# Expert stage of a decoder layer: the sum of row names moves from VectorE to GpSimd, and scatters lose one of their waits

## The chip, the core and the metric

The kernel runs on one core of a Trainium2 chip. Its engines are TensorE (PE), VectorE (DVE), ScalarE (ACT), GpSimd (POOL) and SyncE (SP, which only issues DMAs here). Each runs its own instructions in order, and they wait for each other through semaphores. The metric is the time of one execution on the device in microseconds (us). Before the change it is 1711.96 us, the median of three runs (1709.74 to 1717.92).

## The reference

One decoder layer on 4096 tokens (64 sequences of 64) of 256 numbers, in float32: self-attention, cross-attention with 16 heads over a context, and a mixture of experts. The change touches the last one alone:

```python
logits = x @ gate_w.T                          # 64 experts
topv, topi = jax.lax.top_k(logits, 8)
rw = softmax(topv)
gu = jnp.einsum('nh,eih->nei', x, gu_w)        # gate and up, 64 wide each
inter = silu(gate) * up * W[:, :, None]
out = jnp.einsum('nei,ehi->nh', inter, dp_w)
out = out + sigmoid(x @ sh_gate1_w.T) * shared_expert(x)
x = layernorm(x + out)
```

Only eight of 64 experts count for a token, so the kernel computes those alone.

## The kernel before

There are three stages. The attention stage goes over 32 tiles of 128 tokens. It ends each tile by routing: every token's row (its 256 numbers, its eight slot numbers, its token number times eight, its shared gate) is scattered by POOL into `slot_scratch` in DRAM, where the rows of one expert lie together. The expert stage then works through 176 steps. Of these 160 are sparse, of two tiles of 128 rows, each tile with one expert; 16 are shared, where the tokens pass the shared expert. The last stage loads, for each token, its eight results from `expert_out_scratch`, weighs and sums them and normalises. Those loads wait for all scatters.

In the expert stage each engine has its own order, written out by hand. PE in round s turns the x rows of step s (`turn_x`, L1664), multiplies by gate and up for step s-1 (`gate_and_up`, L1682), turns the gated product of s-2 (`turn_inner`, L1690) and makes the down products of s-3 (`project`, L1701 and L1703, which signal `y_ready`). ACT copies x out of PSUM (L1741), takes silu (L1748) and copies the turned product (L1756). SP loads the rows of a step eight steps ahead (L1548) and waits in `free_rows` (L1520) until the buffer is free: it wants x turned, y ready and the name taken of eight steps before.

A result row goes to the place token times eight plus the column in which the token holds this slot. DVE works that out in three parts:

- `match_row` (L1806): compares the eight slot numbers of each row with the slot that the row lies in, times the column; two instructions give `matched`.
- `name_row` (L1819): adds the token number to it, `named`, as integers.
- `bound_row` (L1825): keeps 16 bits and adds a large number for rows that the step doesn't own, so that the scatter leaves them out; this is `target`, a ring of eight.

DVE's round s is: match of s, the product of silu and up of s-1 (`gate_inner`, L1840), name of s, copy of y of s-3 out of PSUM (`copy_y`, L1849), bound of s, and in 96 of the rounds a piece of the router's weights (`find_weights`, L1859). The down products of step s wait for the copy of y of step s-1, since they write the same bank.

POOL has nothing in this stage but the scatters (`scatter`, L1617). For each sparse step it issues two indirect DMAs of 128 rows (L1623), after three waits:

```python
pool.wait_ge(sig["y_copied"], s + 1)
pool.wait_ge(sig["row_bounded"], n + 1)
pool.wait_ge(sig["y_ready"], min(s + 2, STEPS))
```

The third is the down products of step s+1. The y buffers are a ring of eight (`HELD`).

Of the kernel before, what the change touches and what calls it, by code (L numbers as in the profile page):

```python
# [11 lines left out]
ALU = mybir.AluOpType  # L12
# [3 lines left out]
P = 128  # L16
# [12 lines left out]
SLOT8, TOK, GATE = D, D + TOP_K, D + TOP_K + 1  # L29
# [11 lines left out]
SPARSE_STEPS = (N * TOP_K // P + EXPERTS) // 2  # L41
STEPS = SHARED_STEPS + SPARSE_STEPS
# [1367 lines left out]
slots_numbered slots_open  # L1410
x_in0 x_in1 x_in2 x_in3 x_in4 x_in5 x_in6 x_in7
x_turned x_copied gate_up_done silu_done gated inner_turned inner_copied y_ready y_copied
row_matched row_named row_bounded
y_stored0 y_stored1 y_stored2 y_stored3 y_stored4 y_stored5 y_stored6 y_stored7
y_scattered0 y_scattered1 y_scattered2 y_scattered3 y_scattered4 y_scattered5 y_scattered6 y_scattered7
slots_as_float w_matched w_kept w_summed
# [3 lines left out]
def expert_phase(nc, sig, end, out, slot_d, row_d, meta_d, y_d, shared_d, place_d, first_d, bound_d, count, jump, w8, gu, dp,  # L1420
                 places, rows, slot_of, weights, scattered, down):

    with ExitStack() as stack:
        def sb(name, shape, dt=F32):
            return stack.enter_context(nc.sbuf_tensor(name, shape, dt))
# [18 lines left out]
        x_in = [sb(f"x_rows{n}", [P, 2, XW]) for n in range(8)]  # L1444
# [8 lines left out]
        part = sb("part", [P, 1])  # L1453
        column = sb("column", [P, TOP_K])
        match = [sb(f"match{n}", [P, 2, TOP_K]) for n in range(2)]
        matched = [sb(f"matched{n}", [P, 2]) for n in range(2)]
        named = [sb(f"named{n}", [P, 2], U32) for n in range(2)]
        targets = sb("targets", [P, 8, 2], U32)
        target = [targets[:, n, :] for n in range(8)]
# [20 lines left out]
        steps_of = {step: s for s, step in enumerate(order)}  # L1480

        def sparse(s):
            return order[s][0] == "sparse"

        def number(s):
            return order[s][1]
# [26 lines left out]
        def _(sp):  # L1513
# [6 lines left out]
            def free_rows(s):  # L1520

                if s >= 8:
                    sp.wait_ge(sig["x_turned"], s - 7)
                    if sparse(s):
                        sp.wait_ge(sig["y_ready"], s - 7)
                    if sparse(s - 8):
                        sp.wait_ge(sig["row_named"], number(s - 8) + 1)
                    else:
                        sp.wait_ge(sig["y_copied"], s - 7)

# [71 lines left out]
        @block.gpsimd  # L1602
        def _(pool):
            nc.gpsimd.memset(identity[:, :], 0.0).then_inc(sig["identity_zeroed3"], 1)
            pool.wait_ge(sig["identity_zeroed3"], 1)
            nc.gpsimd.affine_select(out=identity[:, :], in_=identity[:, :], compare_op=ALU.not_equal, fill=1.0,
                                    base=0, pattern=[[-1, P]], channel_multiplier=1).then_inc(sig["identity_made3"], 1)
            nc.gpsimd.memset(minus_half[:, :], -0.5).then_inc(end["constants4"], 1)

            def fill(out, pattern, base, step):  # L1610
                nc.gpsimd.iota(out, pattern, base=base, channel_multiplier=step,
                               allow_small_or_imprecise_dtypes=True).then_inc(sig["numbered"], 1)

            fill(part[:, :], [[0, 1]], 0, 1)
            fill(column[:, :], [[1, TOP_K]], 0, 0)

            def scatter(s):  # L1617
                n = number(s)
                pool.wait_ge(sig["y_copied"], s + 1)
                pool.wait_ge(sig["row_bounded"], n + 1)  # L1620
                pool.wait_ge(sig["y_ready"], min(s + 2, STEPS))
                for j in range(2):
                    nc.gpsimd.indirect_dma_start(  # L1623
                        out=y_d[:, :],
                        out_offset=bass.IndirectOffsetOnAxis(ap=target[n % 8][:, j:j + 1], axis=0),
                        in_=y[s % HELD][:, j, :], in_offset=None, bounds_check=N * COLS - 1, oob_is_err=False)\
                        .then_inc(sig[f"y_scattered{s % HELD}"], 16)

            for s in range(STEPS):
                if sparse(s):  # L1630
                    scatter(s)
            for n in range(HELD):
                pool.wait_ge(sig[f"y_scattered{n}"], 32 * sum(sparse(s) for s in range(n, STEPS, HELD)))

            def root(t):
                pool.wait_ge(end["var"], t + 1)
                nc.gpsimd.tensor_tensor(rs[:, t % 4:t % 4 + 1], ve[:, t % 4:t % 4 + 1], minus_half[:, :], ALU.pow)\
                    .then_inc(end["rstd"], 1)

            pool.wait_ge(end["constants4"], 1)  # L1640
            for t in range(TILES):
                root(t)
# [146 lines left out]
        def _(dve):  # L1789
# [16 lines left out]
            def match_row(s):  # L1806
                n = number(s)
                dve.wait_ge(*rows_loaded(s))
                if n == 0:
                    dve.wait_ge(sig["slots_numbered"], 1)  # L1810
                if n >= 2:
                    dve.wait_ge(sig["row_named"], n - 1)
                for j in range(2):
                    nc.vector.scalar_tensor_tensor(match[n % 2][:, j, :], x_in[s % 8][:, j, SLOT8:SLOT8 + TOP_K].bitcast(U32),  # L1814
                                                   slot_of[:, 0, 2 * n + j:2 * n + j + 1], column[:, :], ALU.is_equal,
                                                   ALU.mult, accum_out=matched[n % 2][:, j:j + 1])\
                        .then_inc(sig["row_matched"], 1)

            def name_row(s):  # L1819
                n = number(s)  # L1820
                dve.wait_ge(sig["row_matched"], 2 * n + 2)
                nc.vector.tensor_tensor(named[n % 2][:, :], matched[n % 2][:, :], x_in[s % 8][:, :, TOK], ALU.add)\
                    .then_inc(sig["row_named"], 1)

            def bound_row(s):  # L1825
                n = number(s)
                dve.wait_ge(sig["row_named"], n + 1)
                if n == 0:
                    dve.wait_ge(sig["slots_open"], 4)
                if n >= 8:  # L1830
                    dve.wait_ge(*y_free(steps_of["sparse", n - 8]))
                nc.vector.scalar_tensor_tensor(target[n % 8][:, :], named[n % 2][:, :], 0xFFFF,  # L1832
                                               beyond[:, 2 * n:2 * n + 2], ALU.bitwise_and, ALU.bitwise_or)\
                    .then_inc(sig["row_bounded"], 1)
# [24 lines left out]
            def find_weights(n):  # L1859

                t, stage = n // 3, n % 3
                if n % (3 * META_TILES) == 0:
                    part_of = n // (3 * META_TILES)
                    dve.wait_ge(sig["metas_in"], 16 * (part_of + 1))
                    dve.wait_ge(sig["slots_in"], 16 * (part_of + 1))
                    own = slice(t, t + META_TILES)
                    nc.vector.tensor_copy(slots_f[:, own, :], slots[:, own, :]).then_inc(sig["slots_as_float"], 1)
                    dve.wait_ge(sig["slots_as_float"], part_of + 1)
                wide = [P, TOP_K, EXPERTS]
                if stage == 0:  # L1870
                    nc.vector.tensor_tensor(w_match[:, :, :], metas[:, t % (2 * META_TILES), 0:EXPERTS].unsqueeze(1).to_broadcast(wide),
                                            slots_f[:, t, :].unsqueeze(2).to_broadcast(wide), ALU.is_equal)\
                        .then_inc(sig["w_matched"], 1)
                elif stage == 1:
                    dve.wait_ge(sig["w_matched"], t + 1)
                    nc.vector.tensor_tensor(w_match[:, :, :], w_match[:, :, :],
                                            metas[:, t % (2 * META_TILES), EXPERTS:].unsqueeze(1).to_broadcast(wide), ALU.mult)\
                        .then_inc(sig["w_kept"], 1)
                else:
                    dve.wait_ge(sig["w_kept"], t + 1)  # L1880
                    nc.vector.tensor_reduce(w8[:, t, :], w_match[:, :, :], AX.X, ALU.add).then_inc(sig["w_summed"], 1)

            for s in range(STEPS + 3):
                now = s < STEPS and sparse(s)
                if now and number(s) == 0:
                    table_slots()
                if now:
                    match_row(s)
                if 0 <= s - 1 < STEPS:
                    gate_inner(s - 1)  # L1890
                if now:
                    name_row(s)
                if 0 <= s - 3 < STEPS:
                    copy_y(s - 3)
                if now:
                    bound_row(s)
                n = number(s) - 24 if now else None
                if now and 0 <= n < 3 * TILES:
                    find_weights(n)
# [88 lines left out]
```

## Time and profile before

| | |
|---|---|
| median of three runs | 1711.96 us |
| profiled execution | 1717.95 us |
| its span, first to last instruction | 1716.2 us |
| mean granted TensorE clock | 0.939 of 2.4 GHz |
| PE, DVE, ACT, POOL busy | 1461.1, 1134.9, 770.8, 1000.0 us |
| DMA | 247.99 MB, mean 144 GB/s |

The profile's page comes from one execution. An engine's busy time counts its compute instructions, and for POOL its indirect DMAs while they are issued. The attention stage takes about the first 1000 us, the expert stage runs to about 1613, the last stage to the end. "Released by" in a row is worked out from the semaphores; "remote" means that the profile doesn't name the releaser. Ends of matmuls are modelled.

### The profile page before, as it was taken

Reading aid. Unit: us, or ns where it says so; the run is one execution under the profiler, and the core shown is the slowest. Engines: PE = TensorE matmul, PEld = TensorE weight load, DVE = VectorE, ACT = ScalarE, POOL = GpSimd, SP = SyncE. Lnnn points to the kernel's source line nnn. Section 1 sums busy time; section 2 is a strip of 40 time slices with the busy share of each in tenths; the row PEclk is TensorE's granted clock in tenths of the full one; section 3 lists DMA queues with packets and bytes.
Section 4 is the critical chain, followed back from the end, with each engine's and each line's share of the span. In section 5 each row is a group of like instructions: output and inputs, shape, how many; then the busy total and the mean of one; then the engine's idle time right before and its main releaser. Section 6 shows DMA issues by size and latency. Waiting matters only on the chain. (4 is left out here: it accounts for less than half of the span.)

```text
span 1716.2 us, 35026 instructions
## 1 busy us (share of the span) xinstructions
PE 1461.1 (85%) x9324; PEld 1183.5 (69%) x9324; DVE 1134.9 (66%) x3731; ACT 770.8 (45%) x2649; POOL 1000.0 (58%) x991
## 2 busy tenths in 40 slices
PE   3799999999999999999998727877877787887587
PEld 2688888888888888888887625655655555665464
DVE  2568787878778888888887444455555555344398
ACT  2465656565565565555655112322322232232254
POOL 3446777776766776777766424455555555555322
PEclk8799999999999999999999759899899999889799
DMA  7333232323232212122212946656656556554697
GB/s 259 101 119 104 98 117 83 125 78 119 86 111 75 83 58 80 64 74 66 72 64 83 291 150 186 185 173 174 188 168 186 171 170 177 173 172 134 228 417 318
DMA packets 184341, 247.99 MB, mean 144 GB/s; under 512 B 30796, under 2 KB 160921, under 8 KB 179748
## 3 DMA queue, kind: packets, MB, share of 16 engines
q1 hardware_dynamic: 150820, 171.55, 32.7%
q0 software_dynamic: 27648, 69.28, 11.0%
q10 hardware_dynamic: 5760, 5.87, 1.0%
q8 instruction: 45, 0.74, 0.2%
q14 instruction: 68, 0.56, 0.1%
HBM read 136.98 MB, written 117.98 MB: 149 GB/s over the span
## 5 line engine op out<-in xcount | busy, mean ns | idle before, releaser
L1623 POOL DMA_INDIRECT expert_out_scratch<-y,targets x320 | 318.9, 997 | 277.2 <-DVE targets L1832 104.8
L573 POOL DMA_INDIRECT slot_scratch<-xrow x256 | 273.6, 1069 | 194.4 <-issue 90.4
L1682 PE MATMUL bank_g<-gu,x_turned 128*128 (+1 forms) x1408 | 213.6, 299 | 29.8 <-issue 18.8
L1682 PEld LDWEIGHTS bank_g<-gu,x_turned 128*128 128x128 f32 x1408 | 189.2, 209 | 48.7 <-issue 47.8
L1840 DVE TENSOR_TENSOR inter<-silu,bank_g 128x128 f32<-128x128 f32 x176 | 50.3, 286 | 256.9 <-ACT silu L1748 213.4
L1741 ACT ACTIVATE x_turned<-bank_x 128x512 f32<-128x512 f32 x176 | 105.4, 599 | 231.2 <-PE bank_x L1664 144.7
L860 ACT ACTIVATE q_work<-q_work 128x128 f32<-128x128 f32 x512 | 151.1, 298 | 128.9 <-DVE q_work L1058 110.3
L764 PE MATMUL bank_d<-wo_w,o2t 128*128 128x256 f32 x1536 | 194.5, 287 | 3.0 <-DVE o2t L977 3.0
L764 PEld LDWEIGHTS bank_d<-wo_w,o2t 128*128 128x128 f32 x1536 | 188.7, 194 | 3.1 <-DVE o2t L977 3.1
L1701 PE MATMUL bank_y<-dp,inter_t 64*128 (+1 forms) x352 | 132.8, 460 | 49.7 <-DVE y L1849 23.1
L522 POOL TENSOR_TENSOR q_rs<-q_ve,minus_half 128x8 f32<-128x8 f32 x64 | 105.5, 1648 | 89.4 <-DVE q_ve L1048 88.8
L628 PE MATMUL bank_c<-wq_w,x1t 128*128 128x512 f32 x576 | 144.3, 395 | 3.6 <-DVE x1t L977 2.8
L1664 PE MATMUL bank_x<-identity,x_rows 128*128 128x128 f32 x704 | 123.4, 301 | 25.5 <-DMA x_rows<-token_row_scratch 25.5
L1664 PEld LDWEIGHTS bank_x<-identity,x_rows 128*128 128x128 f32 x704 | 79.8, 149 | 88.8 <-issue 88.5
L1849 DVE COPY y<-bank_y 128x512 f32<-128x512 f32 x160 | 110.1, 688 | 46.2 <-PE bank_y L1703 25.8
L1748 ACT ACTIVATE silu<-bank_g 128x128 f32<-128x128 f32 x176 | 49.6, 282 | 191.5 <-PE bank_g L1682 112.9
L1703 PE MATMUL bank_y<-dp,inter_t 64*128 64x256 f32 x352 | 133.3, 461 | 0.0
L729 PE MATMUL bank_c<-k2t,stage_b 128*128 128x64 f32 x1024 | 127.1, 285 | 0.0
L628 PEld LDWEIGHTS bank_c<-wq_w,x1t 128*128 128x128 f32 x576 | 107.7, 191 | 25.5 <-DVE x1t L977 3.2
L729 PEld LDWEIGHTS bank_c<-k2t,stage_b 128*128 128x128 f32 x1024 | 123.4, 201 | 0.6 <-issue 0.3
L1701 PEld LDWEIGHTS bank_y<-dp,inter_t 64*128 64x128 f32 x352 | 56.2, 199 | 84.6 <-issue 82.2
L860 ACT ACTIVATION_READ_ACCUMULATOR q_work<-q_work 128x1 f32 x512 | 96.9, 189 | 0.0
(253 smaller groups left out, 3225.9 us busy)
## 6 DMA issues: line engine op xcount, KB each, us to landing
x_rows<-slot_scratch SPq DMA_DIRECT2D x320, 136.0 KB
results<-expert_out_scratch SPq DMA_DIRECT2D x32, 1024.0 KB, 8.8
slot_scratch<-zeros SPq DMA_DIRECT2D x16, 816.0 KB, 4.5
dp<-in_down SPq DMA_DIRECT2D x161, 64.0 KB
slot_scratch<-zeros SPq DMA_DIRECT2D x8, 1088.0 KB, 8.4
gu<-in_gate_up SPq DMA_DIRECT2D x11, 768.0 KB
expert_out_scratch<-y,targets POOLq DMA_INDIRECT x320
token_row_scratch<-xrow SPq DMA_DIRECT2D x32, 136.0 KB
```

Of the source, the lines that this page charges most:

```text
L522: nc.gpsimd.tensor_tensor(out_, base, minus_half[:, 0:width], ALU.pow).then_inc(sig[done], 1)
L573: nc.gpsimd.indirect_dma_start(out=slot_d[:, :], out_offset=bass.IndirectOffsetOnAxis(ap=xrow[slot][:, SLOT8 + k:SLOT8 + k + 1].bitcast(U3 ...
L628: last = nc.tensor.matmul(target, left[a][:, c, :], right(b, c), start=(n == 0 and c == 0), stop=(n == len(PASSES) - 1 and c == C - 1))
L729: last = nc.tensor.matmul(bank_c[:, n, p * S:(p + 1) * S], q2t[:, n, 2 * p:2 * p + 2, :].rearrange("p h s -> p (h s)"), k2t[:, p // 2, n * ...
L764: last = nc.tensor.matmul(bank_d[:, 0, 0:D], o2t[a][:, h, :], wo_w[b][:, h, :], start=(n == 0 and h == 0), stop=(n == len(PASSES) - 1 and ...
L860: last = nc.scalar.activation(q2s[:, h, :], q2[:, h, :], ACT.Square, accum_out=q2_ss[:, h:h + 1])
L1623: nc.gpsimd.indirect_dma_start(out=y_d[:, :], out_offset=bass.IndirectOffsetOnAxis(ap=target[n % 8][:, j:j + 1], axis=0), in_=y[s % HELD][ ...
L1664: mm = nc.tensor.transpose(bank_x[:, s % 2, (2 * j + c) * P:(2 * j + c + 1) * P], x_in[s % 8][:, j, c * P:(c + 1) * P], identity[:, :])
L1682: mm = nc.tensor.matmul(bank_g[:, s % 2, j * P:(j + 1) * P], xt[s % 2][:, j, c, :], w, start=(c == 0), stop=(c == C - 1))
L1701: nc.tensor.matmul(bank_y[:, 0, 0:D], inter_t[s % 2][0:INNER, :], dp[0:INNER, bass.ds(own, D)], start=True, stop=True)
L1703: nc.tensor.matmul(bank_y[:, 1, 0:D], inter_t[s % 2][INNER:P, :], dp[INNER:P, ring * D:(ring + 1) * D], start=True, stop=True).then_inc(si ...
L1849: nc.vector.tensor_copy(y[s % HELD][:, :, :], bank_y[:, :, 0:D])\
```

## The change

POOL makes the sum of token and column (`sum_row`), two sparse steps ahead of the pair that it scatters next, and signals `row_summed`. DVE's `name_row` becomes a clamp of that sum to 0..65535, and it and `bound_row` move to two rounds later. `matched` becomes a ring of eight, and there is a new ring `summed`. The scatters no longer wait for the down products of the next step. SP's `free_rows` waits for `row_summed` in place of `row_named`.

```diff
@@ free_rows (SP)
                     if sparse(s - 8):
-                        sp.wait_ge(sig["row_named"], number(s - 8) + 1)
+                        sp.wait_ge(sig["row_summed"], number(s - 8) + 1)
@@ scatter (POOL)
                 pool.wait_ge(sig["y_copied"], s + 1)
                 pool.wait_ge(sig["row_bounded"], n + 1)
-                pool.wait_ge(sig["y_ready"], min(s + 2, STEPS))
...
-            for s in range(STEPS):
-                if sparse(s):
-                    scatter(s)
+            SUMMED_AHEAD = 2
+
+            def sum_row(n):
+                if n >= SPARSE_STEPS:
+                    return
+                pool.wait_ge(sig["row_matched"], 2 * n + 2)
+                if n >= 8:
+                    pool.wait_ge(sig["row_named"], n - 7)
+                nc.gpsimd.tensor_tensor(summed[:, n % 8, :], matched[:, n % 8, :],
+                                        x_in[steps_of["sparse", n] % 8][:, :, TOK], ALU.add)\
+                    .then_inc(sig["row_summed"], 1)
+
+            for n in range(SUMMED_AHEAD):
+                sum_row(n)
+            for n in range(SPARSE_STEPS):
+                sum_row(n + SUMMED_AHEAD)
+                scatter(steps_of["sparse", n])
@@ match_row, name_row (DVE)
                 if n >= 2:
-                    dve.wait_ge(sig["row_named"], n - 1)
+                    dve.wait_ge(sig["row_matched"], 2 * n - 2)
+                if n >= 8:
+                    dve.wait_ge(sig["row_summed"], (n - 7))
...
-                                                   ALU.mult, accum_out=matched[n % 2][:, j:j + 1])\
+                                                   ALU.mult, accum_out=matched[:, n % 8, j:j + 1])\
...
-                dve.wait_ge(sig["row_matched"], 2 * n + 2)
-                nc.vector.tensor_tensor(named[n % 2][:, :], matched[n % 2][:, :], x_in[s % 8][:, :, TOK], ALU.add)\
+                dve.wait_ge(sig["row_summed"], (n + 1))
+                nc.vector.tensor_scalar(named[n % 2][:, :], summed[:, n % 8, :], 0.0, 65535.0, ALU.max, ALU.min)\
                     .then_inc(sig["row_named"], 1)
@@ find_weights (DVE)
                 if stage == 0:
+                    dve.wait_ge(sig["w_summed"], t)
@@ DVE's rounds
-                if now:
-                    name_row(s)
+                named_now = s - 2 >= 0 and s - 2 < STEPS and sparse(s - 2)
+                if named_now:
+                    name_row(s - 2)
                 if 0 <= s - 3 < STEPS:
                     copy_y(s - 3)
-                if now:
-                    bound_row(s)
+                if named_now:
+                    bound_row(s - 2)
```

## Rows read from the trace of the kernel before

**Rows 1.** L1623, the scatters: the page's part 5, then instructions and who waited.
```profile
L1623 POOL DMA_INDIRECT expert_out_scratch<-y,targets x320 | 318.9, 997 | 277.2 <-DVE targets L1832 104.8
...
L1623 POOL DMA_INDIRECT expert_out_scratch<-y,targets x320: 971/972/1383, 1035.4 to 1611.8; - x160
...
who waited for it (us, times):
```

**Rows 2.** Busy time of each engine in a window of the expert stage.
```profile
core 0: us, PE busy (x) PEld busy (x) DVE busy (x) ACT busy (x) POOL busy (x), PEclk, DMA share, GB/s
1030.00:1606.00 576.00, 455.53 (x2925) 330.37 (x2924) 286.40 (x1404) 169.31 (x516) 313.66 (x315) 0.93 0.58 171
```

**Rows 3.** Waits from 1030 to 1606 us: total, times, longest.
```profile
POOL expert_out_scratch L1623 <- DVE targets L1832: 104.8, 43, 18.7
...
POOL expert_out_scratch L1623 <- remote: 65.3, 32, 2.3
...
ACT x_turned L1741 <- remote: 36.1, 11, 6.0
...
POOL expert_out_scratch L1623 <- PE bank_y L1703: 33.7, 21, 4.2
...
POOL expert_out_scratch L1623 <- DVE y L1849: 5.1, 7, 1.8
```

**Rows 4.** Timeline of a stall: start, us, engine, line; idle before in brackets.
```profile
1203.02 0.66 PE L1664 MATMUL bank_x<-identity,x_rows 128*128 128x128 f32 x4
...
1205.21 0.97 POOL L1623 DMA_INDIRECT expert_out_scratch<-y,targets  x1 [0.30 <-issue]
1205.24 0.66 PE L1664 MATMUL bank_x<-identity,x_rows 128*128 128x128 f32 x4
...
1206.49 0.97 POOL L1623 DMA_INDIRECT expert_out_scratch<-y,targets  x1 [0.30 <-issue]
...
1208.02 0.60 ACT L1741 ACTIVATE x_turned<-bank_x 128x512 f32<-128x512 f32 x1 [5.18 <-remote]
1208.74 2.07 PE L1682 MATMUL bank_g<-gu,x_turned 128*128 x8 [2.84 <-issue]
...
1209.79 0.97 POOL L1623 DMA_INDIRECT expert_out_scratch<-y,targets  x1 [2.32 <-remote]
```

**Rows 5.** Timeline around the first pair of scatters.
```profile
1031.67 0.69 DVE L1849 COPY y<-bank_y 128x512 f32<-128x512 f32 x1
...
1034.09 0.38 PE L1703 MATMUL bank_y<-dp,inter_t 64*128 64x256 f32 x1
...
1035.39 1.00 POOL L1623 DMA_INDIRECT expert_out_scratch<-y,targets  x1 [18.75 <-DVE targets L1832]
```

**Rows 6.** Timeline around the last pair of scatters.
```profile
1605.88 0.69 DVE L1849 COPY y<-bank_y 128x512 f32<-128x512 f32 x1 [1.50 <-PE bank_y L1703]
...
1609.24 0.97 POOL L1623 DMA_INDIRECT expert_out_scratch<-y,targets  x1 [0.30 <-issue]
1610.51 0.97 POOL L1623 DMA_INDIRECT expert_out_scratch<-y,targets  x1 [0.30 <-issue]
```

**Rows 7.** POOL's instructions by form: busy us, mean ns, idle before.
```profile
L548 POOL TENSOR_TENSOR q_work<-q_work,q_rs 128x1024 f32<-128x1024 f32 x32 | 60.7, 1897 | 2.5
...
L522 POOL TENSOR_TENSOR h_rs<-h_ve,minus_half 128x1 f32<-128x1 f32 x64 | 37.7, 589 | 16.9 <-DVE h_ve L984 16.5
...
L1611 POOL IOTA part<- 128x1 f32 x1 | 0.1, 131 | 0.0
```

**Rows 8.** Two lines of DVE: ns at the least, median, most.
```profile
L1822 DVE TENSOR_TENSOR named<-matched,x_rows x160: 148/155/230, 1025.5 to 1597.4; 128x2 uint32<-128x2 f32 x160
...
L1017 DVE TENSOR_SCALAR p1n<-p,p_rec x32: 286/457/479, 32.4 to 900.4; 128x128 f32<-128x128 f32 x32
```

**Rows 9.** Timeline of a longer scatter.
```profile
1216.77 0.69 DVE L1871 TENSOR_TENSOR w_match<-metas,slots 128x512 f32<-128x512 f32 x1
1216.92 1.38 POOL L1623 DMA_INDIRECT expert_out_scratch<-y,targets  x1 [1.62 <-DVE targets L1832]
...
1218.61 0.97 POOL L1623 DMA_INDIRECT expert_out_scratch<-y,targets  x1 [0.30 <-issue]
```

More of the change, by code:

```diff
@@ L1412 @@
 x_turned x_copied gate_up_done silu_done gated inner_turned inner_copied y_ready y_copied
-row_matched row_named row_bounded
+row_matched row_summed row_named row_bounded
 y_stored0 y_stored1 y_stored2 y_stored3 y_stored4 y_stored5 y_stored6 y_stored7
@@ L1455, in expert_phase @@
         match = [sb(f"match{n}", [P, 2, TOP_K]) for n in range(2)]
-        matched = [sb(f"matched{n}", [P, 2]) for n in range(2)]
+        matched = sb("matched", [P, 8, 2])
+        summed = sb("summed", [P, 8, 2])
         named = [sb(f"named{n}", [P, 2], U32) for n in range(2)]
```

## The prediction

> **What bounds the kernel now.** I read the page first. In its second part the expert stage stands out (from about 1000 us on): PE falls from nines to sevens and eights, and DMA doubles. The costliest group of the page belongs to this stage: POOL's 320 indirect DMAs, two for each of 160 sparse steps [rows 1]. Next the stage's window from 1030 to 1606 us: POOL is busy 313.7 of 576 us, PE 455.5, DVE 286.4, ACT 169.3, and the granted clock is 0.93 [rows 2]. With 176 steps in the stage (160 sparse, 16 shared) a step takes about 3.3 us. No engine is full: PE stands still for 120.5 us, POOL for 262.3 us.
>
> Then the waits. POOL's come before the first scatter of a pair: 104.8 + 65.3 + 33.7 + 5.1 = 208.9 us in 103 of 160 pairs; ACT stands 36.1 us on something the profile doesn't name [rows 3]. The timeline shows what a stall looks like. PE's four turns of x end at 1205.90, yet ACT, which needs them alone, starts at 1208.02, 2.1 us late, and PE's next product only at 1208.74. All that time POOL runs scatters back to back; its last ends at 1207.46, the signals come through about a microsecond later, and the next pair starts at 1209.79 [rows 4]. So the stage is bound by a loop of short dependent steps over PE, ACT and DVE whose signals arrive late while POOL and its scatters are at work. Two numbers rule it: how long POOL's work covers a step, and how late each signal is.
>
> Nothing waits for POOL: the list of who waited for the scatters is empty [rows 1]. Eight y buffers and eight targets keep it free.
>
> **The wait that goes.** A pair waits for its own y (copied by DVE) and for the down products of the next step, and those products wait for the same copy, so the second event is always the later one. First pair: y's copy runs 1031.67 + 0.69 = 1032.36, the next products end at 34.09 + 0.38 = 1034.47, and the scatter starts at 1035.39, so 0.92 us after its last condition [rows 5]. Without the wait it could start at 1032.36 + 0.92 = 1033.28, 2.1 us earlier. I did this for each pair: earliest start = the later of (own copy's end + 0.92) and (end of the pair before + 0.30, the gap inside a pair). The last pair gains nothing: the pair before ends at 1610.21 and it starts at 1610.51 [rows 6]. Over pairs 2 to 160 POOL's removable idle is 130 us, in 83 pairs more than 0.3 us.
>
> That is not yet time of the kernel, since nobody waits for POOL. An earlier pair ends earlier, and so the stretch with late signals ends earlier; but that pays only where PE stands too. I take the share of PE's idle in POOL's idle, 120.5 / 262.3 = 0.46: 130 x 0.46 = -60 us. The bounds are 0 (nobody waits for POOL) and -130. At the end of the stage the results are loaded only when the last scatter has landed, and POOL runs behind: last copy ends at 1606.57, last pair starts 3.9 us later [rows 6]. With each pair earlier I take -2 us there (0 to -3.1).
>
> **The sum that POOL takes over.** 160 adds of 128x2. No such add is in the trace: a 128x1 fill takes 0.131 us, a 128x1 power 0.589, and an add or product of 128x1024 1.897 [rows 7]. I take 0.30, between the small ones, and 0.08 for its gap, as before the large products (2.5 us for 32 [rows 7]). Where POOL stood idle anyway the add lies in the idle time; where pairs ran back to back, 76 by my count, it is paid: 76 x 0.38 = +29 us. Bounds: 76 x 0.21 = +16, 160 x 0.67 = +107.
>
> **The names on DVE.** The DVE add (0.155 us) becomes a clamp of the same size [rows 8]; 0 +/- a few us, beneath DVE's 290 us of idle [rows 2]. It moves two steps later, with the bound, but still ahead of that step's copy of y, so the scatter doesn't wait for it. The new waits on match (sum of eight steps before, match of two before) and on w_summed rest on things long done, and so does SP's wait for the sum: two steps later than the name, of eight. Nothing for these. But the clamp now waits for POOL, in front of the copy of y. POOL adds for step m+3 only after it has issued the scatters of step m, and DVE copies y of step m+2 only after the clamp of m+3. That closes a circle that was open. Uncongested it takes 0.92 (copy to scatter), 2.25 (the pair [rows 4]), 0.38 (add), about 0.2 to be seen, 0.16 (clamp) and 0.69 (copy) = 4.6 us for two steps, below the 6.6 that two steps take now. I charge 40 late clamps at 0.2 = +8 us (0 to +80, as below).
>
> **The sum.** -60 - 2 + 29 + 8 = -25 us. The profiled execution took 1717.95 us (1.75 around its span of 1716.2), near the top of the three runs (1709.74 to 1717.92); it becomes 1693. On the median of 1711.96 that is 1687 us.
>
> **A rule of the skill.** Row first: the scatter that started at 1216.92, while a DVE product of two SBUF tiles ran (1216.77 to 1217.46), took 1.38 us and the next one 0.97 [rows 9]. The Trainium skill, "SBUF — State Buffer", "Who interferes with whom", says that a VectorE instruction with two SBUF inputs keeps a GpSimd one that reads SBUF out for its whole length, and that a VectorE instruction in a 2-port mode (its list has tensor_scalar, which the clamp is) and a GpSimd one shut each other out. By the first part this trace agrees; on the clamp it speaks against the change, and becomes the third rival.
>
> **Rivals.** (1) *The new circle binds: slower.* The clamp stands behind POOL's pair, and signals are late exactly then. With one signal late by 2.1 us, as in [rows 4], in place of the 0.2, the circle takes 6.5 us, or 3.25 a step, no better than now; with y's signal late by 0.5 as well 7.0, 3.5 a step: 160 x 0.2 = +32 us, 1744 us. It decides from a total lateness of some 2 us a turn. For it: POOL would need 2.25 + 0.30 + 0.38 = 2.9 us of the 3.3 of a step, so it has little room to catch up, and PE's bursts at 2.2 us a step (turns of x at 1203.02 and 1205.24 [rows 4]) would be cut. Against: in the windows where POOL is idle signals are prompt.
>
> (2) *Nothing comes of either.* Starting earlier only moves the pairs to another phase of the step: each pair is released by the copy instead of by the next products, one step on, and the same number of late signals meets the loop. Then the adds hide in the idle and it stays at 1712, within 0.5%. For it: nobody waits for POOL [rows 1].
>
> (3) *The clamp is shut out by the scatters.* The nearest rows are DVE's products by a scalar in SBUF, 0.286 us at the least and 0.457 in the median [rows 8]: +0.17 each for 160 is +27 us; at worst a whole scatter, 0.97. Half of it lies in DVE's idle, so +13 us, 1725; shut out for a whole scatter at every third step, +50.
>
> **Chances.** Forecast 0.45, rival 1 0.30, rival 2 0.15, rival 3 0.10. The likeliest case's own range is 1665 to 1703 (the 0.46 from 0.3 to 0.65). The range goes from 1650 (the gain without the costs) to 1750 (rival 1 with a little more): a case where all 130 us are gained, or where the clamp loses a scatter each time, is left out. 0.5% (8.6 us) is about what can be told from no change here: faster 0.45, same 0.18 (rival 2 and the edges of the others), slower 0.37.
>
> **What would show it.** Right: POOL's waits before a pair fall from 209 us to under 120; the pairs' first scatter follows its own copy by about 0.9 us; the add takes about 0.3 us; PE's idle in the stage falls below 100 us; the last scatter starts within 3 us of the last copy. Rival 1: the clamp's line appears with idle before it released by POOL's add, over 60 us in all, and PE's down products wait longer on the copy of y. Rival 2: PE's idle stays near 120 us though POOL's waits shift. Rival 3: clamps of 0.3 us and more, or start late with no release. Wrong altogether: if the stage's length doesn't follow PE's idle, or if the time moves in the attention stage, whose code is the same.

## The result

The change made the kernel slower: 1743.46 us (median of 4 runs, 1739.6 to 1749.75) against 1714.94 for the kernel before (4 runs, 1709.74 to 1718.53), a ratio of 1.0155 [1.0125, 1.0185]. The forecast of 1687 had the wrong sign. The range held the time, and it is the figure of the first rival almost to the microsecond, but the cause was another one, as the experiments show. The profiled execution took 1749.75 us.

The page of the changed kernel, its first part and the lines that answer to [rows 1] and to DVE's copy of y (line, engine, operation, out<-in, count; busy us, mean ns of one; idle before it and its releasers):

```profile
PE 1485.0 (85%) x9324; PEld 1203.8 (69%) x9324; DVE 1141.7 (65%) x3731; ACT 774.6 (44%) x2649; POOL 1038.8 (59%) x1151
...
L1623 POOL DMA_INDIRECT expert_out_scratch<-y,targets x320 | 319.8, 999 | 250.7 <-DVE y L1865 126.7
```

The changed kernel, the stage from the first to the last of the 160 sparse copies of y, and a window of the attention stage (columns as in [rows 2]):

```profile
1037.90:1638.80 600.90, 467.57 (x2912) 342.06 (x2912) 291.22 (x1399) 172.10 (x513) 352.40 (x473) 0.89 0.55 164
100.00:900.00 800.00, 780.23 (x5275) 677.01 (x5274) 647.35 (x1701) 463.69 (x1740) 561.91 (x527) 0.99 0.25 84
```

The same two windows of the kernel before:

```profile
1031.70:1605.90 574.20, 453.83 (x2912) 329.17 (x2911) 285.22 (x1396) 168.27 (x513) 313.56 (x315) 0.93 0.58 171
100.00:900.00 800.00, 780.20 (x5317) 677.43 (x5314) 651.56 (x1712) 462.67 (x1742) 563.28 (x528) 1.00 0.26 85
```

The attention stage is the same (PE 780.2 us in both). The spans differ by 31.8 us: the copies run over 26.7 us more, and the first one comes 6.2 us later, which is no part of the change (over the runs below it lies between 1023 and 1042 us, whatever the kernel). Of the 26.7 us, PE's idle time takes 13.0 (120.4 to 133.3) and its busy time 13.7, with the same 2912 matmul records at a lower granted clock, 0.89 for 0.93. Most of the idle time is new at one place: before the down products PE stands 78.7 us in all, where it was 49.6; before the gate products it fell from 27.7 to 13.6.

Where PE's idle time comes from stands in the waits from 1030 to 1640 us. The changed kernel (total, times, longest):

```profile
POOL expert_out_scratch L1623 <- DVE y L1865: 126.7, 58, 3.0
...
POOL expert_out_scratch L1623 <- DVE targets L1848: 53.9, 18, 4.9
...
DVE y L1865 <- remote: 46.5, 28, 3.3
PE bank_y L1715 <- DVE y L1865: 42.1, 33, 2.6
...
ACT x_turned L1755 <- remote: 40.1, 19, 3.4
...
ACT silu L1762 <- remote: 30.3, 16, 4.1
...
DVE y L1865 <- PE bank_y L1717: 27.0, 40, 2.1
...
POOL expert_out_scratch L1623 <- DVE named L1838: 2.2, 2, 1.9
```

The kernel before, the same waits around the copy of y, and ACT's before silu:

```profile
ACT silu L1748 <- remote: 63.4, 30, 3.9
...
DVE y L1849 <- PE bank_y L1703: 25.8, 39, 1.5
...
PE bank_y L1701 <- DVE y L1849: 23.1, 23, 1.8
...
DVE y L1849 <- remote: 11.5, 13, 1.7
```

POOL waits less before a pair, 126.7 + 53.9 + 2.2 = 182.8 us where [rows 3] add up to 208.9. But DVE's copy of y waits 46.5 us on something unnamed, where it was 11.5, and PE's down products wait 42.1 us for that copy, where it was 23.1. ACT's silu went the other way, 30.3 us on something unnamed where it was 63.4. The new instructions themselves, by their lines (ns at the least, median, most):

```profile
L1637 POOL TENSOR_TENSOR summed<-matched,x_rows x160: 197/218/770, 1032.0 to 1636.0; 128x2 f32<-128x2 f32 x160
its engine sat idle before it (us, times) until:
  DVE match L1830: 10.9, 3
who waited for it (us, times):
  DVE named L1838: 1.0, 1
```

```profile
L1838 DVE TENSOR_SCALAR named<-summed x160: 154/161/420, 1035.5 to 1636.2; 128x2 uint32<-128x2 f32 x160
```

DVE's clamp waited for POOL's add once, for 1.0 us: the circle of rival 1 did not bind. How an add lies between pairs (start, us, engine, line; idle before in brackets):

```profile
1200.91 1.19 POOL L1623 DMA_INDIRECT expert_out_scratch<-y,targets  x1 [0.30 <-issue]
...
1202.10 0.22 POOL L1637 TENSOR_TENSOR summed<-matched,x_rows 128x2 f32<-128x2 f32 x1
...
1202.49 1.00 POOL L1623 DMA_INDIRECT expert_out_scratch<-y,targets  x1 [0.16 <-issue]
```

From scatter to scatter 0.39 us pass (1202.10 to 1202.49) where 0.30 do without an add; over the pairs that stand back to back the median is 0.392 with an add and 0.305 without. Most of the add fits into a gap that was there, and 0.09 us of POOL's cadence is its price.

### The profile page after: what moved, and what is told of

Its sections match the earlier page's. It is cut to its first block and busy times, and to the rows that moved or that the text cites. A ratio compares the mean times of both kernels' runs of the same rounds, so it can differ in the third digit from the quotient of the medians.

```text
span 1748.0 us, 35342 instructions
## 1 busy us (share of the span) xinstructions
PE 1485.0 (85%) x9324; PEld 1203.8 (69%) x9324; DVE 1141.7 (65%) x3731; ACT 774.6 (44%) x2649; POOL 1038.8 (59%) x1151
## 5 line engine op out<-in xcount | busy, mean ns | idle before, releaser
L1623 POOL DMA_INDIRECT expert_out_scratch<-y,targets x320 | 319.8, 999 | 250.7 <-DVE y L1865 126.7
L1696 PE MATMUL bank_g<-gu,x_turned 128*128 (+1 forms) x1408 | 220.5, 307 | 15.5 <-issue 13.3
L1696 PEld LDWEIGHTS bank_g<-gu,x_turned 128*128 128x128 f32 x1408 | 197.6, 217 | 30.9 <-issue 30.3
L1715 PE MATMUL bank_y<-dp,inter_t 64*128 (+1 forms) x352 | 139.9, 482 | 78.7 <-DVE y L1865 42.1
L1865 DVE COPY y<-bank_y 128x512 f32<-128x512 f32 x160 | 110.1, 688 | 81.1 <-remote 46.5
L1717 PE MATMUL bank_y<-dp,inter_t 64*128 64x256 f32 x352 | 140.4, 483 | 0.0
L729 PEld LDWEIGHTS bank_c<-k2t,stage_b 128*128 128x128 f32 x1024 | 126.7, 205 | 0.6 <-issue 0.3
```

What stands on the lines that cost most here:

```text
L729: last = nc.tensor.matmul(bank_c[:, n, p * S:(p + 1) * S], q2t[:, n, 2 * p:2 * p + 2, :].rearrange("p h s -> p (h s)"), k2t[:, p // 2, n * ...
L1623: nc.gpsimd.indirect_dma_start(out=y_d[:, :], out_offset=bass.IndirectOffsetOnAxis(ap=target[n % 8][:, j:j + 1], axis=0), in_=y[s % HELD][ ...
L1696: mm = nc.tensor.matmul(bank_g[:, s % 2, j * P:(j + 1) * P], xt[s % 2][:, j, c, :], w, start=(c == 0), stop=(c == C - 1))
L1715: nc.tensor.matmul(bank_y[:, 0, 0:D], inter_t[s % 2][0:INNER, :], dp[0:INNER, bass.ds(own, D)], start=True, stop=True)
L1717: nc.tensor.matmul(bank_y[:, 1, 0:D], inter_t[s % 2][INNER:P, :], dp[INNER:P, ring * D:(ring + 1) * D], start=True, stop=True).then_inc(si ...
L1865: nc.vector.tensor_copy(y[s % HELD][:, :, :], bank_y[:, :, 0:D])\
```

## Experiments

**The chips.** The runs fell on chips of two kinds. On chips 3 and 4 the kernel before took 1560.82 us (median of 12 runs) and 1561.1 (of 25), on chip 14 it took 1717.09 and 1717.84 (of 13 and 18), as in the prediction's trace. I call the second kind the late chip: signals there arrive late in the expert stage; on the first kind, the prompt chips, none does. Which chip gave the result's times isn't on record; both of its traces show late signals. Each ratio of an experiment is against the kernel before on the same chip. On chip 14 the kernel before was timed but not profiled, so its waits there aren't known. The idle time and the stage are taken between the first and the last sparse copy of y, PE's busy time subtracted from the window's length. The last column is the time from the end of a copy to its first scatter, least / median over the 160 pairs.

| kernel | chip | ratio [95%] | stage us | PE idle us | copy to scatter us |
|---|---|---|---|---|---|
| before (prediction's trace) | late | 1 | 574.2 | 120.4 | 1.81 / 3.59 |
| after | late | 1.0155 [1.0125, 1.0185] | 600.9 | 133.3 | 0.78 / 0.78 |
| e1b_no_wait | 14, late | 1.0158 [1.0139, 1.0178] | 596.8 | 135.3 | 0.77 / 0.78 |
| e3b_add_on_dve | 14, late | 1.0130 [1.0108, 1.0152] | 594.3 | 134.0 | 0.77 / 0.78 |
| e7_unread_add_no_wait | 14, late | 1.0142 [1.0110, 1.0174] | 591.8 | 133.2 | 0.78 / 0.78 |
| e6b_unread_add | 14, late | 0.9982 [0.9958, 1.0006] | 566.2 | 108.7 | 1.81 / 3.56 |
| e2b_after_with_wait | 14, late | 0.9992 [0.9967, 1.0017] | 568.5 | 123.0 | 1.81 / 3.20 |
| e9_wait_next_copy | 14, late | 1.0234 [1.0208, 1.0260] | 600.5 | 138.9 | 3.14 / 4.80 |
| e10_wait_turn | 14, late | 0.9994 [0.9973, 1.0016] | 564.5 | 109.6 | 2.39 / 3.82 |
| r1_before | 3, prompt | 1 | 412.3 | 13.7 | 2.36 / 7.86 |
| r2_after | 3, prompt | 1.0090 [1.0057, 1.0124] | 432.4 | 24.5 | 0.78 / 2.02 |
| e5_ahead3 | 3, prompt | 1.0085 [1.0063, 1.0107] | 427.8 | 23.2 | 0.78 / 4.68 |
| e6_unread_add | 3, prompt | 1.0110 [1.0078, 1.0141] | 427.8 | 24.1 | 2.36 / 9.17 |
| e1_before_no_wait | 4, prompt | 0.9977 [0.9949, 1.0005] | 408.9 | 12.8 | 0.78 / 6.86 |
| e2_after_with_wait | 4, prompt | 1.0283 [1.0229, 1.0337] | 458.3 | 43.8 | 1.81 / 2.04 |
| e3_add_on_dve | 4, prompt | 0.9999 [0.9972, 1.0027] | 406.9 | 11.7 | 0.78 / 4.46 |
| e4_clamp_after_copy | 4, prompt | 1.0065 [1.0032, 1.0097] | 425.8 | 20.6 | 0.78 / 3.40 |

**First series: the wait, the add and the circle apart.** All four fell on a prompt chip. e1 is the kernel before without the wait, e2 the changed kernel with it put back:

```diff
                 pool.wait_ge(sig["row_bounded"], n + 1)
-                pool.wait_ge(sig["y_ready"], min(s + 2, STEPS))
```

> The kernel before with one edit: the scatters' wait for the down products of the next step is gone. Circle theory (the loss is DVE's clamp waiting for POOL ahead of the copy of y): no circle here, so it is not slower than before, 1690 to 1715 us. Pacing theory (the removed wait kept the pairs out of the part of a step where late signals hurt): the whole loss is here, 1735 to 1750 us. POOL-time theory (the add lengthens POOL's work): no add here, 1712 us or less.

> The changed kernel with the scatters' wait for the next step's down products put back. Circle theory: POOL gets to its add still later, so the loss stays or grows, 1745 to 1790 us. Pacing theory: the loss goes, 1712 to 1720 us. POOL-time theory: about as after, 1740 us.

e3 is the changed kernel with the add on DVE again (later by two steps, as the clamp was), POOL's `sum_row` gone:

```diff
-                dve.wait_ge(sig["row_summed"], (n + 1))
-                nc.vector.tensor_scalar(named[n % 2][:, :], summed[:, n % 8, :], 0.0, 65535.0, ALU.max, ALU.min)\
+                dve.wait_ge(sig["row_matched"], 2 * n + 2)
+                nc.vector.tensor_tensor(named[n % 2][:, :], matched[:, n % 8, :], x_in[s % 8][:, :, TOK], ALU.add)\
```

> The changed kernel with the add on DVE again (one instruction in the place of the clamp, two rounds later than before), POOL only scatters; the removed wait stays removed. Circle theory: the loss goes, 1690 to 1715 us, and DVE's idle before its copy of y falls from about 81 us back to 43. Pacing theory: the loss stays, about 1740 us. POOL-time theory: the loss goes.

e4 puts DVE's clamp behind the copy of y, which takes the copy out of the circle:

```diff
-                if named_now:
-                    name_row(s - 2)
                 if 0 <= s - 3 < STEPS:
                     copy_y(s - 3)
+                if named_now:
+                    name_row(s - 2)
```

> The changed kernel with the clamp behind DVE's copy of y in the round, not ahead of it. Circle theory: the copy no longer waits for POOL, most of the loss goes, 1705 to 1725 us. Pacing theory: about 1740 us. POOL-time theory: about 1740 us.

Measured: 0.998, 1.028, 1.000 and 1.007. Here the wait alone brings nothing that can be told (0.998 without it), and the loss comes with the adds on POOL: gone with the add on DVE, still 0.7% with the copy out of the circle. The wait and the circle together are worst. But these are ratios of a kernel that takes 1561 us, not 1715, so they could not speak for the result yet. Both kernels were profiled on such a chip.

> The kernel before, for its trace on the same chip as the runs beside it. If this chip is like the one of the first four experiments (about 1561 us), its expert stage takes about 415 us with scatters back to back and PE idle under 20 us; if it is like the one of the prediction (about 1712 us), 578 us and PE idle 121 us.

> The changed kernel, to have it beside its parts. Circle theory: between the version whose clamp stands behind the copy (ratio 1.0065) and the one with the wait put back (1.028), so 1.01 to 1.025 of before on either chip. Pacing theory: no more than 1.005 on the fast chip, where taking the wait away gave 0.998.

The kernel before on the prompt chip, the stage and its waits (1030 to 1640 us):

```profile
1035.30:1447.60 412.30, 398.58 (x2912) 299.66 (x2912) 296.59 (x1396) 178.82 (x513) 310.42 (x310) 0.99 0.79 237
```

```profile
ACT x_turned L1741 <- PE bank_x L1664: 152.9, 165, 2.3
...
DVE y L1849 <- PE bank_y L1703: 5.1, 12, 1.0
```

And its timeline, POOL's scatters with one turn of x between them:

```profile
1199.51 0.97 POOL L1623 DMA_INDIRECT expert_out_scratch<-y,targets  x1 [0.30 <-DVE y L1849]
...
1200.59 0.66 PE L1664 MATMUL bank_x<-identity,x_rows 128*128 128x128 f32 x4
...
1200.79 0.98 POOL L1623 DMA_INDIRECT expert_out_scratch<-y,targets  x1 [0.31 <-PE bank_y L1703]
...
1201.28 0.60 ACT L1741 ACTIVATE x_turned<-bank_x 128x512 f32<-128x512 f32 x1 [0.88 <-PE bank_x L1664]
...
1202.07 0.98 POOL L1623 DMA_INDIRECT expert_out_scratch<-y,targets  x1 [0.31 <-issue]
```

Turns of x end at 1201.25 and ACT starts 0.03 us later, in the middle of back-to-back scatters; in [rows 4] the same hop took 2.1 us. Over the 176 turns it takes 0.04 us in the mean here and never more; in the prediction's trace it takes 1.01 us in the mean, and 68 of them are above 1 us. Nothing waits on "remote" at all. With PE idle for 13.7 us only, POOL is the limit: from the first scatter to the end of the last it takes 422.4 us, of which 320.7 are busy and 319 gaps of 0.305 us make 97.3, and 155 of 159 pairs start so close behind the one before. The price of an add follows: 160 x 0.09 = 14.4 us, 0.9% of 1561, and r2's ratio is 1.009. The attention stage is alike on both kinds (PE 779.2 us in the window from 100 to 900 us). The late chip's stage is longer by 161.9 us, of which 106.7 are idle time of PE and 55.2 busy time. The granted clock is lower too, 0.93 for 0.99; by the ratio of the two clocks that would be some 28 us of the 55 (an estimate), and where the rest comes from isn't shown.

**Second series: whose the add's price is.** e5 adds three steps ahead in place of two, which gives the circle a step more. e6 is the kernel before with an add that nobody reads, so without any circle:

```diff
-            SUMMED_AHEAD = 2
+            SUMMED_AHEAD = 3
```

```diff
...
+                    nc.gpsimd.tensor_tensor(spare[:, number(s) % 8, :], column[:, 0:2], column[:, 2:4], ALU.add)\
+                        .then_inc(sig["spare_made"], 1)
```

> The changed kernel with POOL's adds three sparse steps ahead in place of two. The circle then spans three steps: the clamp of step m+4 waits for the scatters of step m. Circle theory: most of the loss goes, ratio 1.000 to 1.007 to before. POOL-time theory: no change against after, 1.01 to 1.025.

> The kernel before with an add of 128x2 on POOL ahead of each pair, from constants into a tile that nobody reads; no wait on it by any other engine, all else as before. It adds the same work to POOL and no circle. Circle theory: 0.998 to 1.003 of before. POOL-time theory: the loss of after, 1.01 or more.

The wider circle helps nothing (1.0085 for 1.009), and the unread add alone costs as much as the change (1.011): on a prompt chip it is POOL's time, not the circle. In r2 DVE's clamp does wait for POOL, and the copies don't suffer from it:

```profile
DVE named L1838 <- POOL summed L1637: 68.9, 91, 1.8
...
DVE y L1865 <- PE bank_y L1717: 2.6, 7, 1.4
```

**Third series: on the late chip.** The result itself needed the same edits where signals are late. e1b, e2b, e3b and e6b are the kernels above unchanged; e7 is e6 without the `y_ready` wait.

> The kernel before without the wait for the next step's down products once more. On a chip without late signals 0.998 as before. On a chip with late signals: circle theory 0.99 to 1.003; pacing theory 1.012 to 1.02.

> The version with the add on DVE and no wait for the next step once more. On a chip without late signals 1.000 as before. On a chip with late signals: circle theory 0.995 to 1.005; pacing theory (the removed wait) 1.012 to 1.02.

> The kernel before with the unread add on POOL once more, the wait kept. On a chip without late signals 1.011 as before. On a chip with late signals POOL has 264 us of idle in the stage: circle theory 0.998 to 1.004, POOL-time theory 1.01 or more.

> The kernel before without the scatters' wait for the next step's down products, and with an add on POOL ahead of each pair that nobody reads: all that POOL has in the changed kernel, without the circle over DVE. In the first seven experiments no signal was late (PE's turn of x to ACT's copy 0.04 us each time) and POOL ran back to back; there the add's 0.09 us a pair alone gives 1.009 to 1.012, and this should be 1.008 to 1.012. On a chip with late signals, as in the two traces of the result: circle theory 0.995 to 1.005, POOL-and-pacing theory 1.012 to 1.02.

> The changed kernel with the wait for the next step's down products put back, once more. On a chip without late signals 1.028 as before. On a chip with late signals: if the removed wait is the whole loss, 0.995 to 1.005; if the circle over DVE costs too once pairs start later, 1.01 or more.

Each of the four kernels without the wait is slower by 1.3 to 1.6%, each of the two with it is at 1, whatever else they do; so the removed wait is the whole loss, and neither the add nor the circle costs time that shows. That the circle costs nothing is the weaker half of it. In e2b DVE stands 104.3 us before its clamp, of which the profile puts 13.6 down to POOL's add and names nothing for the rest:

```profile
DVE named L1839 <- issue: 90.7, 71, 2.4
...
DVE named L1839 <- POOL summed L1638: 13.6, 10, 1.9
```

PE is idle for 123.0 us there, against 108.7 in e6b, which has the same add and no circle; the granted clock in the stage was 0.965 for 0.919 and PE's busy time 445.6 us for 457.5, which takes most of it back. All ten runs of e2b show the higher clock (0.939 to 0.956 over the whole program, the kernel before 0.922 to 0.935); what raises it isn't shown.

The kernel before without the wait, the stage and its waits:

```profile
1033.50:1630.30 596.80, 461.47 (x2912) 338.27 (x2912) 287.91 (x1395) 172.36 (x513) 314.02 (x316) 0.90 0.55 164
```

```profile
POOL expert_out_scratch L1622 <- DVE y L1848: 195.5, 77, 7.2
...
DVE y L1848 <- remote: 57.0, 33, 3.2
...
PE bank_y L1700 <- DVE y L1848: 55.1, 35, 2.8
```

e6b, which has the add and keeps the wait:

```profile
1041.80:1608.00 566.20, 457.48 (x2912) 330.26 (x2911) 287.17 (x1395) 170.29 (x513) 357.81 (x472) 0.92 0.58 173
```

```profile
PE bank_y L1707 <- DVE y L1855: 23.7, 26, 1.6
...
DVE y L1855 <- remote: 13.5, 13, 1.7
```

Between these two, on one chip, the stage differs by 30.6 us, and PE's idle time by 26.6 of them. A stall in e1b shows what happens:

```profile
1217.52 0.38 PE L1702 MATMUL bank_y<-dp,inter_t 64*128 64x256 f32 x1
1217.83 0.66 PE L1663 MATMUL bank_x<-identity,x_rows 128*128 128x128 f32 x4
...
1218.11 0.97 POOL L1622 DMA_INDIRECT expert_out_scratch<-y,targets  x1 [0.31 <-issue]
...
1219.38 0.97 POOL L1622 DMA_INDIRECT expert_out_scratch<-y,targets  x1 [0.31 <-issue]
1221.25 0.69 DVE L1848 COPY y<-bank_y 128x512 f32<-128x512 f32 x1 [2.36 <-remote]
1221.31 0.60 ACT L1740 ACTIVATE x_turned<-bank_x 128x512 f32<-128x512 f32 x1 [2.09 <-remote]
...
1222.21 0.47 PE L1700 MATMUL bank_y<-dp,inter_t 64*128 x1 [2.73 <-DVE y L1848]
```

The down products end at 1217.90, and the pair's first scatter starts 0.21 us later. DVE starts the copy at 1221.25, 3.35 us after the products' end, though it stood idle for 2.36 us; ACT, which needs the turns of x (ended 1218.49), starts at 1221.31. Both come 0.9 us after the second scatter's end (1220.35), and PE waits 2.73 us for the copy.

Is it the signal that is late, or do the products really end later than the model says? The trace also holds the moment at which each semaphore was updated (a tenth to a fifth of those of PE's products are missing on the late chip). In this stall four of PE's products end at 1217.90, 1218.48, 1219.38 and 1219.49, and their updates stand at 1221.23, 1221.29, 1221.38 and 1221.42: ends spread over 1.59 us, updates within 0.19. Of the 68 updates of the down products in e1b that come more than 1 us late, 54 have another late update of PE within 0.2 us. So the signals are held up and then come through together. On the prompt chips an update follows its product's end by 0.02 us.

The same records say how often that happens, and who stands idle over it (late chips, between the first and the last sparse copy; "late" is an update more than 1 us behind the end of the down products):

| kernel | old wait | late / recorded | mean us late | DVE idle before copies of y, us | PE idle before down products, us |
|---|---|---|---|---|---|
| before | kept | 65 / 150 | 1.05 | 44.4 | 49.6 |
| e6b | kept | 61 / 157 | 0.96 | 46.9 | 45.9 |
| e2b | kept | 64 / 159 | 0.79 | 28.8 | 83.2 |
| e10 | moved to a turn | 54 / 145 | 0.99 | 56.2 | 51.7 |
| after | gone | 69 / 146 | 1.16 | 91.0 | 78.7 |
| e1b | gone | 68 / 151 | 1.15 | 97.1 | 80.6 |
| e3b | gone | 69 / 150 | 1.15 | 98.0 | 79.4 |
| e7 | gone | 68 / 146 | 1.23 | 88.3 | 73.2 |
| e9 | moved to a copy | 63 / 153 | 1.12 | 115.8 | 96.0 |

One would expect that the old wait kept POOL still while the signal of the next down products travelled. The records don't bear that out: with the wait 65 of 150 came late, without it 68 of 151, and the products ended while POOL was inside a pair in 123 of the 150 and in 126 of the 151. The signals are only somewhat later without it. What changes most is who stands idle: before its product with silu DVE waits less (240.0 us before, 207.6 in e1b), before the copy of y twice as long, and PE's down products wait for that copy. (In e2b they wait as long, but there DVE stands before its clamp.) Why the late signals meet the copy once pairs follow their own copy directly isn't shown; it remains an interpretation that it is the phase of POOL's pairs in the step of the others.

**Fourth series: delay or phase?** If a later start as such was what helped, any later event would do. e9 waits for the next copy of y, so that a pair starts as soon behind a copy as without the wait, one step on; e10 waits for a turn of x:

```diff
-                pool.wait_ge(sig["y_ready"], min(s + 2, STEPS))
+                pool.wait_ge(sig["y_copied"], min(s + 2, STEPS))
```

```diff
-                pool.wait_ge(sig["y_ready"], min(s + 2, STEPS))
+                pool.wait_ge(sig["x_turned"], min(s + 6, STEPS))
```

> The kernel before with the pair's third wait on the copy of y of the next step in place of its down products, some 0.8 us later. Phase theory (what matters is that the signal of the down products is out before POOL starts): 0.995 to 1.005 on a chip with late signals. If any later start is better still, below 0.99. If the place before is an optimum by chance, above 1.01. On a chip without late signals POOL is full and runs behind: 1.00 to 1.01.

> The kernel before with the third wait on PE's turn of x of step s+5, which follows the next step's down products on PE by 0.6 us and whose signal goes to ACT. Phase theory: now both signals, of the down products and of the turned x, are out before POOL starts, and on a chip with late signals this is as fast as before or faster, 0.985 to 1.000. If only the down products' signal matters, 0.998 to 1.005. On a chip without late signals 1.000 to 1.005.

e9 starts latest of all on this chip (4.80 us in the median) and is the slowest, 1.023; e10 starts at 3.82 us and is level with the kernel before. The waits of e9:

```profile
DVE y L1849 <- remote: 55.7, 32, 3.4
PE bank_y L1701 <- DVE y L1849: 50.5, 34, 2.7
```

and of e10:

```profile
PE bank_y L1701 <- DVE y L1849: 36.2, 33, 2.3
...
DVE y L1849 <- remote: 17.8, 16, 2.8
```

So the amount of delay doesn't order these kernels, and the event that a pair waits for does. A start tied to a copy of y, this step's or the next one's, leaves the copy 46 to 59 us on "remote"; one tied to products or turns leaves it 11 to 18. The waits of ACT's copy of x on "remote" go the same way in part: 83.2 us in e9, 55.3 in e1b, 42.1 in e10, 36.1 in [rows 3]; in the changed kernel they are 40.1, hardly more. Those before silu don't: 33.6 in e9, 20.4 in e1b, 35.9 in e10, 63.4 in the kernel before. e10's row of PE (36.2) is above the 23 to 24 of the kernel before and e6b and the time is still level, so that row alone doesn't set it. No version beat both kernels: e1 on the prompt and e6b on the late chip, 0.998 each, can't be told from 1.

What stays open: what holds the signals up. That it is POOL's scatters is inferred, from the updates that come through soon after a pair's end; a kernel whose POOL issues no scatter on the late chip wasn't tried. Nor do the runs show why chips differ.

## Why the prediction was wrong

**What bounds the kernel.** Right: late signals while POOL scatters, in a loop of short steps over PE, ACT and DVE. r1 is the same code without late signals: 1566 us for 1718.

**The wait that goes (-60 us): the step that failed.** POOL's part was about right: the first scatter follows its own copy by 0.78 us (0.92 taken). But "an earlier pair ends earlier, and so the stretch with late signals ends earlier" took for granted that a stretch costs the same wherever it lies. Multiplying POOL's removable idle time by PE's share of idle, 0.46, treated the two as if they lay at random to each other. They don't: in the changed kernel POOL's waits before a pair fell from 208.9 to 182.8 us and PE's idle time in the stage rose from 120.4 to 133.3 us. Alone, the removal is worth +0.0158 x 1717 = +27 us. My bounds, 0 and -130, had no loss in them, because nobody waits for POOL; [rows 4] had shown ACT held up during the scatters with nobody waiting for them. By what path POOL's earlier start costs the others more is known only so far as the table of the third series goes.

**The add (+29 us).** It takes 0.218 us in the median (0.30 taken) but only 0.09 of POOL's cadence (0.38 taken), and on the late chip even that doesn't show: e6b 0.998. The price showed only where POOL is the limit, 14 us on the prompt chips.

**The late clamps (+8 us) and rival 1.** Over 60 us of the clamp waiting for POOL's add was the condition; it was 1.0 us. The other half of the condition, PE waiting longer for the copy of y, came true (23.1 to 42.1), from the removed wait. The time of 1744 agrees by chance: e1b has no clamp and no POOL add and runs to the same ratio, 1.0158 for 1.0155. The circle exists where signals are prompt (68.9 us in r2), and costs where the old wait is kept too (e2, 1.028); on the late chip e2b has it, with 104.3 us of idle time before the clamp, at 0.999. So even over 60 us of idle time before the clamp need not show as lost time.

**Rival 2.** Its argument was close: the pairs move to another phase, released by the copy, and the number of late signals is nearly the same (65 of 150, then 69 of 146). It took for granted that they then cost the same, and they cost more.

**Rival 3.** Wrong: the clamp takes 0.161 us in the median and 0.420 at most. The Trainium skill, "SBUF — State Buffer", "Who interferes with whom", would have a 2-port VectorE instruction and a GpSimd one shut each other out; this case shows little of it (whether the clamp ran in such a mode isn't shown). Of the 160 clamps 66 ran wholly inside a scatter, with the same median of 0.161 us; 11 of these took over 0.2 us, while none of the 74 that met no scatter took over 0.165. All clamps over 0.2 us together lost 1.8 us. For two-input VectorE work the trace shows more: the five longest adds on POOL, 0.520 to 0.770 us, each ran beside DVE's `w_match` product, and so did every scatter of over 1.1 us (17 in the kernel before), too seldom to weigh.

**The end of the stage (-2 us).** As expected: the last copy of y ends at 1639.50 and the last pair starts at 1641.52, 2.0 us later; it was 3.9. The changed kernel's timeline there:

```profile
1638.81 0.69 DVE L1865 COPY y<-bank_y 128x512 f32<-128x512 f32 x1 [1.44 <-PE bank_y L1717]
...
1641.52 0.97 POOL L1623 DMA_INDIRECT expert_out_scratch<-y,targets  x1 [0.30 <-issue]
```

**What would have shown it.** Of the signs that I named, POOL's waits (182.8 us, not under 120) and PE's idle time (120 to 133 us, not under 100) already spoke against the forecast in the changed kernel's profile; the copy of y on "remote" was not among them, and is the row that told.

## What to carry to other kernels

A wait on which no result depends may still be worth its time, because it sets when an engine's work falls in the step of the others. Before taking it out, ask what will then run beside what, and test the removal alone, and the wait moved to another event, not only the whole change. A rival whose number comes true isn't shown by that: look for its own sign, here the clamp's wait for POOL.

## What the runs showed of the hardware

- Chips differ. The same kernel takes 1561 us on two chips and 1717 on another, with the attention stage alike (PE 779.2 and 780.2 of 800 us) and all of the difference in the stage where POOL's scatters run beside short dependent steps (412 for 574 us). An edit's sign can differ with them: the wait's removal is 0.998 on one kind and 1.016 on the other, the added POOL work 1.011 and 0.998.
- On the late chip a signal from PE to ACT or DVE can take 2 to 3.4 us while POOL issues indirect DMAs, and signals so held up come through together (four within 0.19 us in the stall shown); on the others it takes 0.04 us beside the same scatters.
- Between two indirect DMAs on POOL lies a gap of 0.30 us; a 128x2 add put into it makes it 0.39, though it takes 0.218 itself.
- An indirect DMA of 128 rows takes 0.97 us on POOL; every one of over 1.1 us (up to 1.38 in the kernel before, 17 of 320) ran beside a DVE product of 128x512 with two inputs.
